# Experts' first product with the weights standing still and the activations moving; each block's first weights fetched from DRAM on their own

## What is computed

```python
x = x + _L0_xattn_ref(_layernorm(x), ctx_1024, ctx_1024, ...)
x = x + _L0_ffn_ref(_layernorm(x), router_weight, router_bias, gate_up_proj, gate_up_bias, down_proj, down_bias)
x = x + _L1_xattn_ref(ctx_1024, _layernorm(x), mask, ...)
x = x + _L1_ffn_ref(_layernorm(x), Wg, W1, b1, W2, b2)
```

```python
# layer 0 (ff = 512)
gu   = flat @ gate_up_proj[e] + gate_up_bias[e]          # 256 -> 1024
gate = minimum(gu[:512], 7);  up = clip(gu[512:], -7, 7)
act  = (up + 1) * gate * sigmoid(1.702 * gate)
down = act @ down_proj[e] + down_bias[e]                 # 512 -> 256
# layer 1 (ff = 1024)
h    = gelu(xe @ W1[e] + b1[e])                          # 256 -> 1024
ye   = h @ W2[e] + b2[e]                                 # 1024 -> 256
```

## Time and profile before

| | us |
|---|---|
| median of 3 runs | 2267.36 (2264.06 to 2269.27) |
| the profiled execution | 2280.04 |
| its span, first to last instruction | 2278.1 |
| TensorE busy in the span | 2009.3 (88%) |
| VectorE, ScalarE, POOL busy | 1247.1, 908.7, 620.3 |
| mean granted TensorE clock, as a share of 2.4 GHz | 0.931 |
| `m0e`: first matmul to last `y` | 353.9 to 592.4 |
| `m1e`: first matmul to last `y` | 1930.8 to 2249.7 |

### The profile page before, as it was taken

How to read it: one execution, slowest core, us unless ns; L and a number is a source line. 1 busy time by engine, 2 the same in 40 slices (tenths; PEclk the granted TensorE clock), 3 DMA queues, 4 the chain that set the end, 5 groups by cost and what they waited for, 6 DMA issues and landing times. The chain is left out here.

```text
span 2278.1 us, 37556 instructions
## 1 busy us (share of the span) xinstructions
PE 2009.3 (88%) x12252; PEld 1551.9 (68%) x12253; DVE 1247.1 (55%) x2957; ACT 908.7 (40%) x1746; POOL 620.3 (27%) x571
## 2 busy tenths in 40 slices
PE   4788957999449999999999999999999974999994
PEld 2477944666237887887788887878788753666673
DVE  4273054666606676666676667767677654222223
ACT  2543412222215555454555555555555530322221
POOL 1300002333155323432343224432343001122220
PEclk9897958999659999999999999999999995999997
DMA  5501173111222122112221122112221119111113
GB/s 189 166 34 71 60 291 106 46 45 45 87 68 56 35 61 67 44 42 49 66 50 42 41 66 66 45 37 53 67 50 42 34 37 372 54 32 33 34 34 123
DMA packets 93660, 167.51 MB, mean 74 GB/s; under 512 B 22129, under 2 KB 54575, under 8 KB 91451
## 3 DMA queue, kind: packets, MB, share of 16 engines
q1 hardware_dynamic: 82875, 142.65, 21.8%
q0 software_dynamic: 8320, 20.65, 3.0%
q10 hardware_dynamic: 2304, 2.10, 0.3%
HBM read 79.90 MB, written 32.41 MB: 49 GB/s over the span
## 5 line engine op out<-in xcount | busy, mean ns | idle before, releaser
L1823 DVE TENSOR_REDUCE a_part_peak<-a_slot 128x1 f32<-128x512 f32 (+1 forms) x512 | 354.9, 731 | 312.1 <-PE a_slot L1648 311.4
L1785 ACT ACTIVATE a_probT<-a_slot 128x640 f32<-128x640 f32 x256 | 180.2, 704 | 476.0 <-PE a_slot L1657 258.1
L1648 PE MATMUL a_slot<-a_KHL,a_QHL 128*128 128x512 f32 (+1 forms) x1536 | 346.0, 361 | 19.5 <-DVE a_probT L1846 9.8
L1648 PEld LDWEIGHTS a_slot<-a_KHL,a_QHL 128*128 128x128 f32 x1536 | 273.5, 191 | 119.4 <-issue 52.4
L1773 ACT ACTIVATE a_prob<-a_slot,a_npeak 128x1024 f32<-128x1024 f32 x256 | 284.0, 1109 | 3.9 <-DVE a_npeak L1825 3.9
L1673 PE MATMUL a_po<-a_probT,a_V 128*64 128x256 f32 (+1 forms) x2304 | 277.0, 385 | 0.0
L1657 PE MATMUL a_slot<-ident,a_prob 128*128 128x128 f32 x2048 | 267.1, 274 | 0.0
L1657 PEld LDWEIGHTS a_slot<-ident,a_prob 128*128 128x128 f32 x2048 | 236.0, 143 | 8.5 <-issue 0.2
L1600 PE MATMUL a_side<-a_W,a_latT 128*128 128x128 f32 x1536 | 204.9, 286 | 24.9 <-DVE a_KT L1833 10.4
L1673 PEld LDWEIGHTS a_po<-a_probT,a_V 128*64 128x64 f32 (+1 forms) x2304 | 153.7, 136 | 87.3 <-issue 21.7
L1600 PEld LDWEIGHTS a_side<-a_W,a_latT 128*128 128x128 f32 x1536 | 191.1, 200 | 31.1 <-DVE a_KT L1833 15.0
(11 more groups left out here) (314 smaller groups left out, 3059.5 us busy)
## 6 DMA issues: line engine op xcount, KB each, us to landing
a_KHL<-a_KT SPq DMA_DIRECT2D x128, 256.0 KB, 4.5
a_QHL<-a_QT SPq DMA_DIRECT2D x128, 128.0 KB, 2.3
m_up<-_L_ffn_gate_up_proj_dram SPq DMA_DIRECT2D x8, 1024.0 KB, 9.5
m_up<-in_L_ffn_W_dram SPq DMA_DIRECT2D x8, 1024.0 KB, 8.6
m_down<-in_L_ffn_W_dram SPq DMA_DIRECT2D x8, 1024.0 KB, 14.1
a_prob_dram<-a0p_zeros SPq DMA_DIRECT2D x4, 1632.0 KB
a_dist_dram<-a_dist SPq DMA_DIRECT2D x4, 1632.0 KB, 8.1
a_band_prob<-a_prob_dram SPq DMA_DIRECT2D x4, 1632.0 KB, 6.7
```

Of the source, the lines that this page charges most:

```text
L1648: ins = t_.matmul(out[:, lo:hi], q, KHL[:, pair.parity, h, part, lo:hi], start=part == 0, stop=part == 1)
L1785: a_.activation(probT[:, u // 4 % 2, HALF:KT_TILES, h, u % 2 * P:(u % 2 + 1) * P], slot[u % 2][:, HALF * P:KT_TILES * P].rearrange("p (t q ...
L1823: v.tensor_reduce(part[:, i:i + 1], slot[u % 2][:, lo:hi], AX.X, ALU.max).then_inc(part_peaked, 1)
```

## The change

In the mixtures the first product is turned: a 128x128 piece of the weights stands, the 128 columns of `xT` move, and the result comes out with the hidden dimension on the partitions. 8 pieces x 2 chunks make 16 matmuls of 128 columns. The result is then already laid out as the second product's stationary operand, so the transposes `paT`, the copy `aT` and one body of the pipeline (s ends at 39) go. `py` has two buffers. The bias has one value per partition and piece and is spread by the access pattern. The first weights are no longer loaded in `front`: SP reads each block's expert number and fetches 1 MB from DRAM into one of four buffers `w`, as soon as the block four before it has used it. The wait for `down` is in body 1, where it was in body 2; the block of `experts` ends without draining GpSimd. In the preparation of layer 0's attention `context.sync` is SP's first work.

```diff
@@ preparation of layer 0's attention
             def _(sp):
+                context.sync(sp)
                 sp.wait_ge(tails, 1)
                 ...
                 for n in range(NN):
                     sp.dma_start(prob_d[n]..., zeros[:, :]).then_inc(cleared, 16)
-                context.sync(sp)
@@ front
             load_constants(sp)
-            load_weights(sp, 0)
             for t in range(TILES):
                 ...
-            load_weights(sp, 1)
+            load_weights(sp)
@@ experts
+        w = sb("w", [P, GATHERS, EC, UP])
+        w_loaded = [sem(f"w_loaded{q}") for q in range(GATHERS)]
-        aT = sb("aT", [P, 2, FC, P])
-        paT = ps("paT", [P, max(FC, 4), P])
-        py = ps("py", [P, BANK])
+        py = [ps(f"py{i}", [P, BANK]) for i in range(2)]
-        block = ctx.enter_context(nc.Block())
+        block = ctx.enter_context(nc.Block(no_gpsimd_drain=True))
@@ SP
+            def fetch(b):
+                if b >= GATHERS:
+                    sp.wait_ge(h_done, b - GATHERS + 1)
+                e = sp.value_load(lists["expert"][0:1, b:b + 1], min_val=0, max_val=NE - 1)
+                sp.dma_start(w[:, b % GATHERS, :, :], wup[bass.ds(e, 1)].rearrange("a (c p) n -> p (a c) n", p=P)
+                             ).then_inc(w_loaded[b % GATHERS], 16)
+            for b in range(2):
+                fetch(b)
             load_rest(sp)
+            for b in range(2, BLOCKS):
+                fetch(b)
             after.sync(sp, scattered)
@@ TensorE
-                if isinstance(s, int) and s == 2:
+                if isinstance(s, int) and s == 1:
                     pe.wait_ge(*down_ready)
                 if within(s):
-                    e = pe.value_load(lists["expert"][0:1, bass.ds(s, 1)], min_val=0, max_val=NE - 1)
+                    pe.wait_ge(w_loaded[r], (s - r) * (16 // GATHERS) + 16)
                     ...
-                    for half in range(UP // BANK):
+                    for k in range(UP // P):
+                        cols = slice(k * P, (k + 1) * P)
                         for c in range(EC):
-                            ins = nc.tensor.matmul(ph[:, q, cols], xT[:, c, :], up[:, bass.ds(e, 1), c, cols]...,
+                            ins = nc.tensor.matmul(ph[:, q, cols], w[:, r, c, cols], xT[:, c, :],
                                                    start=c == 0, stop=c == EC - 1)
-                if within(s - 1):
-                    pe.wait_ge(a_done, s)
-                    reached(pe, aT_out, s - 1)
-                    for f in range(FC):
-                        ins = nc.tensor.transpose(paT[:, f, :], a[:, 1 - q, f * P:(f + 1) * P], ident[:, :])
-                    ins.then_inc(aT_done, 1)
                 if within(s + 1):
                     turn_x(s + 1, (r + 1) % GATHERS)
-                if within(s - 2):
+                if within(s - 1):
                     ...
-                        ins = nc.tensor.matmul(py[:, 0:E], aT[:, q, f, :], down[...], ...)
+                        ins = nc.tensor.matmul(py[1 - q][:, 0:E], a[:, 1 - q, f * P:(f + 1) * P], down[...], ...)
@@ ScalarE
-                    nc.scalar.activation(aT[:, 1 - q, :, :], paT[:, 0:FC, :], ACT.Copy).then_inc(aT_out, 1)
@@ VectorE
-                    v.tensor_tensor(h[:, q, :], ph[:, q, :], bup[:, bass.ds(e, 1), :]..., ALU.add)
+                    v.tensor_tensor(h[:, q, :].rearrange("p (k n) -> p k n", n=P), ph[:, q, :].rearrange(...),
+                                    bup[:, bass.ds(e, 1), :]....unsqueeze(2).to_broadcast([P, UP // P, P]), ALU.add)
@@ mixture
-            up = sb("up", [P, NE, EC, E * 4])
-            bup, bdown = sb("bup", [P, NE, E * 4]), sb("bdown", [P, NE, E])
+            bup, bdown = sb("bup", [P, NE, 4 * E // P]), sb("bdown", [P, NE, E])
-            def load_weights(sp, stage):
-                ...
+            def load_weights(sp):
+                sp.dma_start(bup[:, :, :], I[wbup]).then_inc(up_loaded, 16)
+                load_down(sp, range(NE - lent))
```

More of the change, by code:

```diff
@@ L966, in _, with experts @@
             s.after(v.tensor_tensor(lists["gather"][:, :], code[:, :], wrap[:, :], ALU.add))
-def experts(nc, name, layer, ident, lists, xn_rows, y_rows, up, down, bup, bdown, up_ready, down_ready, load_rest, ff, follow):
+def experts(nc, name, layer, ident, lists, xn_rows, y_rows, wup, down, bup, bdown, up_ready, down_ready, load_rest, ff, follow):
     FC = ff // P
@@ L991, in experts @@
         ph = ps("ph", [P, 2, UP])
-        paT = ps("paT", [P, max(FC, 4), P])
-        py = ps("py", [P, BANK])
+        py = [ps(f"py{i}", [P, BANK]) for i in range(2)]
         gathered = [sem(f"gathered{q}") for q in range(GATHERS)]
         scattered = sem("scattered")
-        xT_done, xT_out, h_done, h_out, a_done, aT_done, aT_out, y_done, y_out = (
-            sem(n) for n in ("xT_done", "xT_out", "h_done", "h_out", "a_done", "aT_done", "aT_out", "y_done", "y_out"))
+        xT_done, xT_out, h_done, h_out, a_done, y_done, y_out = (
+            sem(n) for n in ("xT_done", "xT_out", "h_done", "h_out", "a_done", "y_done", "y_out"))
         step, gate_ready, sig_ready = sem("step"), sem("gate_ready"), sem("sig_ready")
         after = follow(ctx, h, a, ph)
-        block = ctx.enter_context(nc.Block())
+        block = ctx.enter_context(nc.Block(no_gpsimd_drain=True))
         def steps(engine, body):
@@ L1011, in steps @@
                     body(i * GATHERS + (begin + k), (begin + k) % GATHERS)
-            for s in range(end, BLOCKS + 2):
+            for s in range(end, BLOCKS + 1):
                 body(s, s % GATHERS)
@@ L1066, in body @@
                         for c in range(EC):
[L1067 to L1070, removed]
+                            ins = nc.tensor.matmul(ph[:, q, cols], w[:, r, c, cols], xT[:, c, :], start=c == 0, stop=c == EC - 1)
@@ L1083, in body @@
                     reached(pe, y_out, s - 2)
                     for f in range(FC):
-                        ins = nc.tensor.matmul(py[:, 0:E], aT[:, q, f, :],
+                        ins = nc.tensor.matmul(py[1 - q][:, 0:E], a[:, 1 - q, f * P:(f + 1) * P],
                                                down[:, bass.ds(e, 1), f, :].rearrange("p a n -> p (a n)"),
@@ L1133, in body @@
                     dve.wait_ge(h_done, s + 1)
-                    reached(dve, a_done if layer == 0 else aT_done, s - 1)
-                    v.tensor_tensor(h[:, q, :], ph[:, q, :], bup[:, bass.ds(e, 1), :].rearrange("p a n -> p (a n)"),
+                    reached(dve, a_done if layer == 0 else y_done, s - 1)
+                    v.tensor_tensor(h[:, q, :].rearrange("p (k n) -> p k n", n=P), ph[:, q, :].rearrange("p (k n) -> p k n", n=P),
+                                    bup[:, bass.ds(e, 1), :].rearrange("p a k -> p (a k)").unsqueeze(2).to_broadcast([P, UP // P, P]),
                                     ALU.add).then_inc(h_out, 1)
@@ L1146, in body @@
                         v.scalar_tensor_tensor(a[:, q, :], h[:, q, ff:], 1.0, a[:, q, :], ALU.add, ALU.mult).then_inc(a_done, 1)
[L1147 to L1151, removed]
+                if within(s - 1):
+                    e = dve.value_load(lists["expert"][0:1, bass.ds(s - 1, 1)], min_val=0, max_val=NE - 1)
+                    dve.wait_ge(y_done, s)
+                    reached(dve, scattered, (s - 1) * 16)
+                    v.tensor_tensor(y[:, :], py[1 - q][:, 0:E], bdown[:, bass.ds(e, 1), :].rearrange("p a n -> p (a n)"),
                                     ALU.add).then_inc(y_out, 1)
@@ L1361, in mixture @@
             c3.close()
-            experts(nc, f"{name}e", layer, ident, lists, xn_rows, y_rows, up, down, bup, bdown,
-                    (up_loaded, 16 * (NE + 1)), (down_loaded, 16 * (NE + 1)), load_rest, ff,
+            experts(nc, f"{name}e", layer, ident, lists, xn_rows, y_rows, I[wup], down, bup, bdown,
+                    (up_loaded, 16), (down_loaded, 16 * (NE + 1)), load_rest, ff,
                     lambda ctx, h, a, ph: follow(ctx, f"{name}c", gates, y_rows, h, a, ph))
@@ L1957, in lay_out @@
         out[n] = a[n]
-    for n in ("L0_ffn_gate_up_bias", "L0_ffn_down_bias", "L1_ffn_b1", "L1_ffn_b2"):
+    for n in ("L0_ffn_gate_up_bias", "L1_ffn_b1"):
+        out[n] = a[n].reshape(NE, -1, P).transpose(2, 0, 1)
+    for n in ("L0_ffn_down_bias", "L1_ffn_b2"):
         out[n] = a[n].reshape(1, -1)
```

10 lines of the change are left out of this document (3 added, 7 removed).

## The result

The changed kernel takes **2231.40 us** (median of 4 runs, 2227.56 to 2233.40); the kernel before, on the same chip, 2265.71 (4 runs, 2263.99 to 2269.27). The ratio is 0.9845, 95% interval 0.9825 to 0.9864: 34 us less, between 31 and 40. The forecast was 2206, range 2194 to 2228. The direction was right, the size was not: the change brings little more than half of the 61.4 us.

The account below looks back on a forecast made before the run. TensorE alone was taken to bound blocks in both mixtures. Gains of 28.4 (`m1e`), 20.2 (`m0e`), 7.7 (context loads first) and 5.1 us (no drain) sum to 61.4, giving a median of 2206 us, range 2194 to 2228.

Parts of the forecast that it names:

- The context edge: Layer 0's attention starts at 54.7 us instead of 62.37 with `context.sync` first: 7.7 us less, bounds 5.3 and 9.9.
- the place of the wait: Start of the mixtures: body 1's second product waits for `down`; 28.4 us less in `m1e`, 20.2 in `m0e`.
- the half clock that had been priced on the second product: Start of `m1e`: after the wait for `down`, half clock was expected to cost 5.91 - 3.43 = 2.5 us.
- The sign that the prediction had named: TensorE should wait some 6 us before the second product of `m1e`'s block 0 and hardly in `m0e`.
- the pace of the first product: Both mixtures: 32 matmuls of 128 columns at 107 ns each, 3.42 us per block against 3.43; no change taken.
- lower bound nothing: First product in both mixtures: no change, since 512-column instructions already make 107 ns per 128 columns.
- upper bound of 122 ns: First product in both mixtures: 1.95 / 16 = 122 ns per instruction, +0.47 us per block, +37 us over 78 blocks.
- The 0.85 us set aside for a half-clock product: End of `m0e`: the last second product may take 3.58 us instead of 1.89; half of the difference was taken.
- Rival 1: First product in both mixtures: weight loads set the pace; without overlap +207 us, 2413; decides from 132 ns; chance 0.05.
- Rival 2: Loop of `m0e`: fetches delay the scatter; +75 us, 2281, if every block, 2243 if every second; chance 0.10.
- Rival 3: Fixed gains smaller: no drain gain (+5.1), `down` 3 us later, layer 0's preparatory zeros 2.4 later; 2216; chance 0.15.
- Rival 4: First product in both mixtures: small holes, 115 ns instead of 107, +0.26 us per block, +20, 2226; chance 0.10.

Follow-up runs that it names:

- experiment 6: The changed kernel without the fetches of blocks 4 to 38 in each mixture, later blocks reusing the first four's weights: 2230.12 us, ratio 0.9827.
- experiment 3: The kernel before with only GpSimd's drain left out at the end of the mixtures: 2263.88 us, ratio 0.9975.
- experiment 4: The changed kernel with the wait for `down` moved ahead of block 0's second product, on TensorE and VectorE: 2222.42 us, ratio 0.9794.
- experiment 5: The kernel with the wait moved, plus own space for normalized tokens and mask, all `down` loaded in `front`, no wait for it: 2208.38 us, ratio 0.9723.
- experiments 7: The kernel before with its first product cut into 32 matmuls of 128 columns, tokens standing and resident weights moving: 2280.15 us, one run.
- experiment 8: The kernel before with its first product cut into 16 matmuls of 256 columns instead of 8 of 512: 2266.20 us, one run.

## Why the prediction was wrong

**Right.** The transposes vanish whole. The order inside a block and the absence of new waits in the loop hold over all blocks. The fetches are hidden (experiment 6). ScalarE and VectorE stay off the path. The fronts keep their length. The context edge comes at 54.53 us (forecast 54.7), and the drain is worth 5.1 (experiment 3). In `m1e` `down` lets TensorE go 1915.19 - 1890.42 = 24.8 us after the first gather; the forecast's 1948.5 lies 24.6 behind the gather at 1923.9. The end of `m0e` waits 2.36 us for VectorE (forecast 2.3).

**The first step that failed: the place of the wait.** The prediction said "body 1's second product, queued behind TensorE's wait, cannot start earlier". The wait stands at the head of body 1, and its *first* product is queued behind it too. In the diff it is there to be read: `wait_ge(*down_ready)` comes before `if within(s)`. The cost, from the first gather to the first second product:

- `m0e`: 357.43 - 331.16 = 26.3 us, where 365.8 - 347.6 = 18.2 was forecast. `down` was 1.5 us later than forecast and the cold first product (at half clock) with its transposes took 6.6. Together +8.1.
- `m1e`: 1921.28 - 1890.42 = 30.9 us against 24.6, +6.3. But the half clock that had been priced on the second product (+2.5) fell on the first, already counted there: -2.4.

The sign that the prediction had named fails with it. TensorE was to wait some 6 us before the second product of `m1e`'s block 0 and hardly in `m0e`; it waits 11.39 and 6.49 us, before block 1's first product.

Experiments 4 and 5 show it in two steps: the wait moved gives back 3.8 and 3.3 us, the wait taken away 4.8 and 9.6 more. In experiment 4 part of the gain stays away, because the idle time only moves, and with it the half clock onto the next product. So of the 8.1 us of `m0e` only 3.8 hang on the wait's place alone. With the wait where the prediction had it, the first second product still starts 354.52 - 333.8 = 20.7 us after the first gather and not 18.2, and it runs at half clock: the forecast had TensorE arrive together with `down` (365.7 and 365.8) and so had priced neither idle time nor a cold product there.

**The second: the pace of the first product.** The prediction read 107 ns for an instruction of 128 columns out of the earlier trace rows, as 1.71 us from the group's start to the next group's, over 16. The same row read with its tail says otherwise. 1.95 us are 15 steps and one instruction, 0.275 us long (the median of 1248 in the kernel after), so a step is (1.95 - 0.275) / 15 = 111.7 ns. Measured: 3.57 / 32 = 111.6. The hand-over to line 1648 was faster than a step, so start-to-start over a short group was too low by 4%. The 103 ns of the earlier trace rows, from which the prediction said that "loads alone do not hold it back", are too low in the same way: the first step of that group is 31 ns, the later ones 111 to 112. That row told of the very pace that came. With 37 first products behind the start that is 37 x 0.14 = 5.2 us in each mixture. The "lower bound nothing" used columns alone (107 per 128 in a 512-column move) and took for granted that pieces cost what the whole does; experiments 7 and 8 refute that at 128 columns and nearly confirm it at 256. The upper bound of 122 ns held.

**The end of `m0e`.** The 0.85 us set aside for a half-clock product were not needed, and 1.3 us were spent on the last `y` behind the scatter, which the earlier trace rows had shown and the sum left out: +0.5.

The sums close: `m0e` 8.1 + 5.2 + 0.5 = 13.8 of the 13.6 missed, `m1e` 6.3 - 2.4 + 5.2 = 9.1 of 8.9. They close better than they can be known: in the four profiles with the mixtures unchanged `m0e` took 242.7 to 244.4 us. The edges make 0.4 more, 22.9 of the 25.4 us between 2206 and 2231.40; the last 2.5 are placed nowhere. The 38.5 us of the traces lie inside the timed interval (31 to 40).

**The rivals.** Rival 1 (loads that set the pace) is refuted in its price: 111.6 ns are far from its 132, and loads of 192 ns that could not overlap would have made 192. (32 of them are 6.14 us; the prediction has 6.08, which changes 4 us of its 2413.) Its mechanism is not refuted. The rows under experiment 8 speak for a pace set by the loads, 4.4 ns above that of the columns. The ratio taken from the Trainium skill ("TensorE: Matmul & The Clock Gate", Back-to-back issue gap), 81 ns against 56, would have made 155 ns here, an estimate. The trace shows 111.6 against 107.2, a step of 4% and not of 45%. Rival 2 (the scatter holds the loop) happened twice in the 39 blocks of `m0e`, 3.1 us in all, one of them the last. Rival 3 was wrong in the drain and in the zeros. Its `down` 3 us later was too large, 1.5 in `m0e` and 0.2 in `m1e`. Rival 4 came nearest in number (2226), by luck: it had 8 ns per instruction where 4.5 came, and nothing of the wait, which made up the rest. It is not made by holes or by register loads between the groups: inside a group of 32 in `m1e` every step is 109 to 112 ns. The chance of 0.60 for the forecast was too high for a sum in which one wait's place had not been checked line by line against the diff. Each of the two misses alone stays inside the range: the wait is 8.1 + 6.3 - 2.4 = 12.0 us, 2218; the pace 10.4, 2216. The high end, 2228, took the rivals one at a time and had no room for two together.

## What to carry over

When a wait moves or a pipeline loses a stage, write out the list of instructions behind the wait on its engine, in the order of the code: the first of them pays for the wait and for the clock after it. Take an operation's pace from the inside of a long group (end minus start, less one instruction, over the count less one), not from a short group's start to its neighbour's; where the first step differs from the others, as in the earlier trace rows, leave it out as well. And profile the unchanged kernel twice before parts of two profiles are subtracted: here a stage that nobody touched differed by 9 us, in step with the clock that it was granted.

## What the runs showed of the hardware

- An fp32 matmul on a 128x128 standing operand, each with its own weight load, follows the next in 429 ns for 512 columns, 216 for 256 and 111.6 for 128. At 128 columns the pace is the same whichever operand stands and whether or not it was fetched just before (3.57 us for 32 in all three forms).
- Such matmuls with 17, 34 or 51 moving columns step 111 to 112 ns too: below 128 columns fewer moving columns bought no time (rows under experiment 8).
- 238 GB/s of DMA into the on-chip memory beside a full TensorE, instead of 47, cost TensorE nothing that could be measured.
- After idle times of 3.3 to 11.4 us the next 1.9 or 3.6 us of work took 3.4 to 6.5 us, most of it at half clock (granted 0.55 to 0.62); after the 2.36 us at the end of `m0e` it did not (1.99 us, granted 1.00). But in the kernel before a product ran at half clock behind a wait of 1.84 us, 0.66 us of work and 0.20 us of idle time (granted 0.50). So the length of the last wait alone does not tell whether the next product is cold:

```profile
584.13 0.66 PE L1076 MATMUL m0e_paT<-ident,m0e_a 128*128 128x128 f32 x4 [1.84 <-DVE m0e_a L1146]
```

- The block's drain of GpSimd behind indirect DMAs was 5.1 us on the path to the next stage (TensorE idle 7.92 us with it, 2.83 without).
- One stage of unchanged code took from 223.7 to 233.5 us in ten executions, with a mean granted clock of 0.96 in the shortest and 0.90 in the longest.
